# The last stage of a fused decoder kernel: work moved from VectorE to GpSimd and ScalarE, and the next batch's rows prepared between tiles

## The reference, cut to what matters

```python
def _L1_ffn_ref(x, weight, weight_scale, bias):      # x is layernorm(x) here
    amax = jnp.max(jnp.abs(x), axis=-1, keepdims=True)
    x_scale = jnp.maximum(amax, 1e-12) / FP8_MAX     # 448
    qinput = (x / x_scale).astype(FP8)               # float8_e4m3fn
    A = qinput.astype(x.dtype) * x_scale
    Bm = weight.astype(x.dtype) * weight_scale
    return jnp.einsum('bsk,nk->bsn', A, Bm) + bias
```

## Time and profile before

| | us |
|---|---|
| three runs | 3648.0, 3655.38, 3653.69 |
| their median | 3653.69 |
| span of the profiled execution | 3648.2 |
| the last stage in it, from the last residual tile of the fifth (3463.2) to the end | 185.0 |

### The profile page before, as it was taken

One profiled execution on the slowest core, in us unless ns is written; L12 is line 12 of the kernel. 1 busy time (PEld: TensorE's weight loads), 2 busy tenths in 40 slices (PEclk: granted clock), 3 DMA queues, 4 the chain that ended last, 5 costly groups with the idle time before them and its releaser, 6 DMA issues. The chain is left out here.

```text
span 3648.2 us, 78625 instructions
## 1 busy us (share of the span) xinstructions
PE 3088.9 (85%) x31124; PEld 1836.6 (50%) x31124; DVE 2698.1 (74%) x4017; ACT 2360.0 (65%) x4397; POOL 1058.4 (29%) x1854
## 2 busy tenths in 40 slices
PE   6999999978999755899778888998899879998824
PEld 3747474645665543444345554555455545555411
DVE  4748483867897765444469988889888988889688
ACT  3838373766786534333368887778777887788534
POOL 2232323156446234233212222222222222222122
PEclk9999999989999977999999999999999999999956
DMA  4050505175365376344399999999999999999843
GB/s 151 28 146 29 172 5 146 37 249 149 122 201 165 94 251 208 81 119 127 92 220 190 190 199 199 199 202 186 214 196 200 189 214 194 199 201 184 158 158 124
DMA packets 1309823, 582.40 MB, mean 160 GB/s; under 512 B 1144338, under 2 KB 1230994, under 8 KB 1306900
## 3 DMA queue, kind: packets, MB, share of 16 engines
q1 hardware_dynamic: 1305428, 560.60, 69.3%
q0 software_dynamic: 4032, 16.78, 1.2%
HBM read 183.63 MB, written 109.45 MB: 80 GB/s over the span
## 5 line engine op out<-in xcount | busy, mean ns | idle before, releaser
L2296 DVE SCALAR_TENSOR_TENSOR ca_halves<-ca_probs,ca_inv,ca_halves 128x1024 f16<-128x1024 f32 x512 | 655.5, 1280 | 109.9 <-ACT ca_halves L2222 102.4
L2288 DVE TENSOR_REDUCE ca_neg_max<-banks 128x1 f32<-128x1024 f32 x512 | 623.8, 1219 | 64.1 <-PE banks L2066 62.6
L2222 ACT ACTIVATE ca_halves<-ca_probs,ca_inv 128x1024 f16<-128x1024 f32 x512 | 586.6, 1146 | 102.9 <-DMA ca_pt<-ca_halves 99.1
L2214 ACT ACTIVATE ca_probs<-banks,ca_neg_max 128x1024 f32<-128x1024 f32 x512 | 568.7, 1111 | 72.6 <-DVE ca_neg_max L2288 70.7
L2032 POOL TENSOR_SCALAR ca_inv<-ca_total 128x1 f32<-128x1 f32 x512 | 97.5, 190 | 1197.1 <-ACT ca_probs L2214 1197.1
L2066 PE MATMUL banks<-ca_kt,ca_qt 64*128 64x512 f16 x3072 | 381.3, 382 | 48.8 <-ACT ca_probs L2214 47.1
L2088 PE MATMUL banks<-ca_pt,ca_v 128*64 128x256 f16 x6144 | 388.6, 277 | 0.9 <-DMA ca_pt<-ca_halves 0.8
L2088 PEld LDWEIGHTS banks<-ca_pt,ca_v 128*64 128x64 f16 x6144 | 318.6, 111 | 94.2 <-issue 78.4
L2035 POOL TENSOR_TENSOR ca_inv<-ca_inv,ca_minus_one 128x1 f32<-128x1 f32 x512 | 280.3, 548 | 42.6
L2066 PEld LDWEIGHTS banks<-ca_kt,ca_qt 64*128 64x128 f16 x3072 | 132.6, 95 | 238.8 <-issue 95.0
L2047 PE MATMUL banks<-ca_ct,ca_w 128*128 128x512 f16 x768 | 180.5, 386 | 48.1 <-DMA ca_ct<-ctx_part 23.8
(11 more groups left out here) (306 smaller groups left out, 5738.7 us busy)
## 6 DMA issues: line engine op xcount, KB each, us to landing
ca_w<-ca_w_parts SPq DMA_DIRECT2D x32, 768.0 KB, 5.4
wa_v<-v_rows SPq DMA_DIRECT2D x44, 264.0 KB, 4.5
v_rows<-wa_v_stage SPq DMA_DIRECT2D x32, 264.0 KB, 2.2
wa_x<-in_x SPq DMA_DIRECT2D x32, 256.0 KB, 5.3
wa_ring<-in_x SPq DMA_DIRECT2D x32, 256.0 KB, 3.9
x_after_window_attention<-wa_ring SPq DMA_DIRECT2D x32, 256.0 KB, 3.1
ba_tokens<-wa_tok_turned SPq DMA_DIRECT2D x32, 256.0 KB, 3.6
ba_xt<-ba_tokens SPq DMA_DIRECT2D x32, 256.0 KB, 7.2
```

What stands on the lines that cost most here:

```text
L2214: act.activation(probs[:, slot, :], scores(i), ACT.Exp, bias=neg_max[:, slot:slot + 1], accum_out=total[:, slot:slot + 1]).then_inc(exped, 1)
L2222: act.activation(halves[:, slot, 0, :], probs[:, slot, :], ACT.Copy, scale=inv[:, slot:slot + 1]).then_inc(split_hi, 1)
L2288: dve.tensor_reduce(out=neg_max[:, slot:slot + 1], in_=scores(i), axis=X_AXIS, op=ALU.max, negate=True).then_inc(maxed, 1)
L2296: dve.scalar_tensor_tensor(out=halves[:, slot, 1, :], in0=probs[:, slot, :], scalar=inv[:, slot:slot + 1], in1=halves[:, slot, 0, :], op0= ...
```

## The change

All of it lies in `fp8_ffn`. One block takes the place of two. Slots become `FF_SLOTS` = 4, `xn` and the scales hold two batches, and four PSUM banks take the transposes instead of two.

- GpSimd writes the normalised rows, with add and mult of two pointer scalars (a negated mean, made in one more small instruction, and the inverse deviation), widens the 8-bit rounding to bfloat16 (a `tensor_copy`), and adds the bias in the turn to which it belongs.
- ACT makes the shifted row and takes the constant off again, the latter one turn later and straight into `q`. The square is gone.
- DVE marks by the exponent bits of the 8-bit value (one bitwise AND on bytes), and COPY_PREDICATED puts the widened value over `q` where they aren't zero.
- The next batch's work lies between the turns: DVE takes `norm_stats` of two tiles in each of turns 0 to 3, and the maxima of two in each of turns 4 to 7; GpSimd makes two tiles of rows in each of turns 4 to 7.
- SyncE loads a tile of the batch after the next behind each store, where it loaded the next batch's eight in one run.
- The weights are decoded in the same block, behind the statistics of batch 0.

```diff
 @block.sync
+    for t in range(NT):
+        sp.dma_start(n.x[:, t, :], tokens_in(x_in, 0, t)).then_inc(n.x_loaded[t], 16)
+    sp.dma_start(bits8 ...); sp.dma_start(w_scale ...); sp.dma_start(bias ...)
...
+    for t in range(NT):
+        sp.wait_ge(n.xn_ready, t + 1)
+        sp.dma_start(n.x[:, t, :], tokens_in(x_in, 1, t)).then_inc(n.x_loaded[t], 16)
     for b in range(B):
-        if b + 1 < B:
-            sp.wait_ge(n.xn_ready, NT * (b + 1))
-            for t in range(NT):
-                sp.dma_start(n.x[:, t, :], tokens_in(x_in, b + 1, t)).then_inc(n.x_loaded[t], 16)
         for t in range(NT + 1):
             if t < NT:
                 sp.wait_ge(n.res_ready, NT * b + t + 1)
                 sp.dma_start(tokens_in(x_out, b, t), n.ring[:, t, :]).then_inc(n.stored[t], 16)
+            if b + 2 < B and t >= 1:
+                sp.wait_ge(n.xn_ready, NT * (b + 1) + t)
+                sp.dma_start(n.x[:, t - 1, :], tokens_in(x_in, b + 2, t - 1)).then_inc(n.x_loaded[t - 1], 16)
             if t >= 1 and b + 1 < B:
                 sp.wait_ge(n.stored[t - 1], 16 * b + 16 * (n.turn + 1))
                 sp.dma_start(n.ring[:, t - 1, :], tokens_in(x_in, b + 1, t - 1)).then_inc(n.ring_loaded[t - 1], 16)
 @block.gpsimd
+    def moments(b):
+        pool.wait_ge(n.moments, 2 * NT * (b + 1))
+        pool.tensor_scalar(neg_mean[:, :], n.mv[:, :, 0], -1.0, 1.0, ALU.mult, ALU.mult).then_inc(centred, 1)
+        norm_gpsimd(pool, n, b)
...
+    def rows(b, t):
+        pool.tensor_scalar(xn[:, b % 2, t, :], n.x[:, t, :], neg_mean[:, t:t + 1], n.rstd[:, t:t + 1],
+                           ALU.add, ALU.mult).then_inc(n.xn_ready, 1)
+    def widen(b, t):
+        turn = NT * b + t
+        pool.wait_ge(coarsened, turn + 1)
+        if turn >= FF_SLOTS:
+            pool.wait_ge(merged, turn - FF_SLOTS + 1)
+        pool.tensor_copy(wide[:, turn % FF_SLOTS, :], coarse[:, turn % FF_SLOTS, :]).then_inc(widened, 1)
...
+    for b in range(B):
+        for t in range(NT):
+            widen(b, t)
+            if b + 1 < B and t == NT // 2:
+                if b >= 1:
+                    pool.wait_ge(merged, NT * b)
+                moments(b + 1)
+            if b + 1 < B and t >= NT // 2:
+                rows(b + 1, 2 * t - NT)
+                rows(b + 1, 2 * t - NT + 1)
+            add_bias(b, t)
 @block.scalar
+    def grids(b, t):
...
+        act.wait_ge(scaled, b + 1)
+        act.activation(coarse[:, s, :], xn[:, b % 2, t, :], ACT.Copy, scale=half_inv[:, b % 2, t:t + 1], saturate=False)
...
+        act.activation(rounded[:, s, :], xn[:, b % 2, t, :], ACT.Identity, bias=rounder[:, :],
+                       scale=half_inv[:, b % 2, t:t + 1]).then_inc(added, 1)
+    def finer(turn):
...
+        act.activation(q[:, s, :], rounded[:, s, :], ACT.Identity, bias=unround[:, :]).then_inc(fined, 1)
+    for turn in range(NT * B):
+        grids(*divmod(turn, NT))
+        if turn >= 1:
+            finer(turn - 1)
+        if turn >= 2:
+            evacuate(turn - 2)
 @block.vector
+    def mark(b, t):
+        dve.wait_ge(coarsened, NT * b + t + 1)
+        dve.tensor_scalar(is_normal[:, s, :], coarse[:, s, :].bitcast(U8), EXPONENT, None, ALU.bitwise_and).then_inc(marked, 1)
+    def merge(b, t):
+        dve.wait_ge(fined, turn + 1)
+        dve.wait_ge(widened, turn + 1)
+        dve.wait_ge(marked, turn + 1)
+        dve.memset(fences[:, 1:2], 0.0)
+        dve.copy_predicated(q[:, s, :], is_normal[:, s, :], wide[:, s, :]).then_inc(merged, 1)
...
+    for b in range(B):
+        for t in range(NT):
+            turn = NT * b + t
+            mark(b, t)
+            if b + 1 < B:
+                if t < NT // 2:
+                    norm_stats(dve, n, b + 1, 2 * t)
+                    norm_stats(dve, n, b + 1, 2 * t + 1)
+                else:
+                    largest_of(b + 1, 2 * t - NT)
+                    largest_of(b + 1, 2 * t - NT + 1)
+                if t == NT // 2 - 1:
+                    norm_aggregate(dve, n, b + 1)
+                if t == NT - 1:
+                    scales(b + 1)
+            merge(b, t)
+            if turn >= 3:
+                residual(turn - 3)
```

More of the change, by code:

```diff
@@ L2339 @@
 ROUNDER = 1.5 * 2.0 ** 13
-FINE_BELOW = 2.0 ** -6
+EXPONENT = 0x78
+FF_SLOTS = 4
 def fp8_ffn(nc, consts, psum, x_in, x_out, dram):
@@ L2352, in fp8_ffn @@
+        neg_mean, amax = sb("ff_neg_mean", [P, NT], F32), sb("ff_amax", [P, NT], F32)
+        x_scale, grid_scale = sb("ff_x_scale", [P, 2, NT], F32), sb("ff_grid_scale", [P, 2, NT], F32)
+        half_inv, out_scale = sb("ff_half_inv", [P, 2, NT], F32), sb("ff_out_scale", [P, 2, NT], F32)
         fences = sb("ff_fences", [P, 4], F32)
[L2353 to L2356, removed]
@@ L2365, in fp8_ffn @@
-        flipped, flip_out, projected = sem("ff_flipped"), sem("ff_flip_out"), sem("ff_projected")
[L2366 to L2376, removed]
-                    for t in range(NT):
[L2378 to L2386, removed]
@@ L2519, in _, with project @@
                 norm_aggregate(dve, n, 0)
+                dve.wait_ge(constant, 2)
+                decode()
+                dve.wait_ge(scale_loaded, 16)
+                for t in range(NT):
+                    largest_of(0, t)
+                scales(0)
                 for b in range(B):
-                    rows(b)
-                    shift(b, 0)
                     for t in range(NT):
-                        if t + 1 < NT:
-                            shift(b, t + 1)
+                        turn = NT * b + t
+                        mark(b, t)
                         if b + 1 < B:
-                            norm_stats(dve, n, b + 1, t)
-                        merge(b, t)
-                        if t >= 2:
-                            residual(b, t - 2)
-                        if b + 1 < B and t == NT - 1:
-                            norm_aggregate(dve, n, b + 1)
-                    for t in range(NT - 2, NT):
-                        residual(b, t)
+                            if t < NT // 2:
[8 more added lines that the diff above has]
+                                scales(b + 1)
+                        merge(b, t)
+                        if turn >= 3:
+                            residual(turn - 3)
+                for turn in range(NT * B - 3, NT * B):
+                    residual(turn)
             @block.tensor
             def _(pe):
-                def project(b, t):
-                    if NT * b + t >= 4:
-                        pe.wait_ge(n.res_ready, NT * b + t - 3)
-                    pe.wait_ge(flip_out, NT * b + t + 1)
+                def project(turn):
+                    t = turn % NT
+                    if turn == 0:
+                        pe.wait_ge(decoded, 5)
+                    if turn >= 4:
+                        pe.wait_ge(n.res_ready, turn - 3)
+                    pe.wait_ge(flip_out, turn + 1)
                     for k in range(KC):
```

223 lines of the change are left out of this document (110 added, 113 removed).

## The result

| us | before | after |
|---|---|---|
| median of the runs | 3655.38 (5 runs, 3648.0 to 3660.06) | 3636.41 (5 runs, 3631.28 to 3647.25) |
| ratio of after to before, 95% interval | | 0.9956 (0.9940 to 0.9972) |
| profiled execution: own time, span | span 3648.2 | 3635.97, 3634.2 |
| last residual tile of the fifth stage | 3463.2 | 3464.7 |
| last stage, from there to the end (difference of the unrounded times) | 184.9 | 169.5 |

The interval is 10 to 22 us faster. The profiled executions differ by 14.0 us in span: the last stage is 15.4 us shorter, and the five stages that nobody touched came out 1.5 us longer.

A forecast was written before the change was run, and what follows sets the result against it. DVE was taken to bound the last stage. Periods saving 12.1 us and the head 9.1, less 1.2 lost in the last batch, gave 20.0 us off the median: 3634 us, range 3608 to 3672.

The forecast's parts named there:

- POOL's rows: Normalised rows on GpSimd, turns 4 to 7 and head: 0.62 us each with add and mult, not 2.07 as with subtract.
- The slower rival: GpSimd's rows cost 2.07 us in turns 4 to 7 and the head; time 3680 us; chance 0.20.
- The first half of a period: From half_inv through turns 0 to 3 to the statistics' aggregate, set by DVE: 16.4 us.
- the seam: Between two batches: three ACT instructions after half_inv, before DVE's merge of the last turn can start, 2.0 us.
- The second half: Turns 4 to 7, aggregate to half_inv: set by GpSimd's chain with DVE hidden, 17.0 us.
- The port: DVE's mark and predicated copy wait for GpSimd's running instruction: 0.39 us each, 0.8 us a turn.
- The moved loads: Loads of x behind stores make DVE's statistics in turns 2 and 3 wait: 4.0 us in batches 1 and 2.
- Batch 0: First of three periods, half_inv to half_inv, without waits for moved loads: 33.4 us against 40.1.
- The head: Start of the last stage up to the first half_inv, with no block end behind the loads: saves 9.1 us.
- The last batch: From the last half_inv to the end, no next batch: 33.0 us against 31.8, loses 1.2.
- small interference: Rival: port and loads hardly bite, turns of 2.8 us, periods of 28.3; time 3608 us; chance 0.10.
- a restarting seam: Rival: each period's seam restarts all engines, some 6 us more each; time 3652 us, no change; chance 0.08.

The follow-up runs named there:

- e2: Changed kernel with GpSimd's rows made by subtract of the mean and mult instead of add of the negated mean and mult; median 3680.91 us, ratio to before 1.0067.
- e1: Changed kernel with the loads of x for tiles 3 to 7 issued together behind tile 4's store; last stage 157.2 us, ratio to before 0.9907.
- e3: Changed kernel with GpSimd's bias added to only the first of 512 features, the rest left out; last stage 150.8 us, ratio to before 0.9899.
- e6: Changed kernel with the 8-bit weights loaded and decoded ahead of batch 0's statistics, still in one block; last stage 172.4 us, ratio to before 0.9965.

## Why the prediction was right, and where its sizes were off

The forecast was 3634, the median 3636.41. The steps did less well than the sum: 20.0 us were forecast for the stage, and 15.4 came in the profiled executions. The medians lie 19.0 apart, 3.6 more than the stage saved; that is within the 7 us by which whole times vary, so that the total came this near is in part luck.

**POOL's rows: right, and on the right ground.** The argument was that a pointer is the same for a whole row, so that the excess of 1.45 us had to be the subtraction's. e2 bears it out: with subtract a row costs 2.07 again (the tile of the scalar, which changed with it, apart). The price of add and mult is 0.76, not 0.62, which makes 8 x 0.14 = 1.1 us a period. The Trainium skill, GPSIMD Engine Reference, section 4.1, has one-input elementwise work here at roughly line-rate. The trace comes near that for add and mult (0.77 us a row of 512 elements, where DVE had taken 0.54 before the change) and contradicts it for subtract and mult (2.07), so the rule could not have decided the case. The slower rival, with its place and its 3680, was priced well: e2 gave 3680.91.

**The first half of a period: right without the loads.** Forecast 16.4 us, 16.5 in e1. Its inner terms moved against each other: the seam took 2.3, not 2.0, ACT's shifted row being 0.80 us where I had at most 0.71 from the earlier trace rows; merge and residual behind it took 1.6, not 1.3, that copy being held (1.01); the three turns took 10.4 in e1 (distances of the copies 3.13, 4.06, 3.18), forecast 10.8; the rest took the 2.3 of the forecast.

**The second half: 1 us low.** Forecast 17.0, measured 17.9. Several sizes were off and partly cancelled: the rows 1.1 more; the negated mean 0.50 us instead of 0.2, which with the waits makes 0.4 more; behind the last row 0.3 more, the first short scale instruction being held (0.50 us, 0.17 in e3); against that POOL lost some 2.1 us at the port, not 2.8, and a bias costs 1.20 from start to start, not 1.26. That POOL would set it and DVE be hidden was right (the 3.99 us turns without a gap on POOL).

**The port: right in kind, smaller in the mean.** I took 0.39 us for each of mark and copy. Their means are 0.26 and 0.24 over the clean price, and most of it is POOL's bias, as e3 shows (0.08 and nothing are left without it). The Trainium skill, SBUF — State Buffer, "SBUF: two separate sides", says that of a DVE instruction in a 2-port mode, or with two SBUF inputs (then only against a GpSimd one that reads SBUF), and a GpSimd one, the first to start has the shared ports for its whole length and the other blocks. The trace agrees, in both directions: the copy at 3548.59 ended 0.55 us after the bias did, and the widening at 3549.11 took 1.07 us. The two prices of L1795 in the earlier trace rows fit as well: POOL worked beside both, but in the one of 2.29 us it started 1.0 us after DVE (1450.35 and 1451.36). The mark, with one input, is held as well, up to 1.50 us, which fits the first kind; no run shows in which mode it ran.

**The moved loads: the step that failed, by its size.** Forecast 4.0 us a period, measured 6.6 in waits and 6.3 by e1. The chain was as put, and from the residual to the landing it took 3.2 and 3.3 us for tiles 5 and 6, forecast 3.4. The error was in what DVE does meanwhile: I had let the mark wait 0.8 us at the port there, and it did not (0.41 and 0.42), so tile 5's statistic stood 2.2 instead of 1.6 and tile 6's 3.0 instead of 2.2. Tile 7's load, issued behind a store and two other loads, took 4.0 us from issue to landing, and 1.4 stood in place of 0.3. I had used the same port wait as a cost in one step and as cover in the next, though it need not fall in the turn where cover is wanted.

**Batch 0: not seen.** 31.0 us against 33.4. In its first three turns there is no residual yet (3 x 0.66 = 2.0) and no merge of a turn before at its seam; from half_inv to the next aggregate it took 13.0 us, where e1's other periods took 16.5. I had counted all periods alike.

**The head: 1.2 us short of its gain.** 25.0 us where 23.8 was forecast. The last aggregate was on time; from there to half_inv it took 11.4, forecast 9.8; 1.1 of the difference is the price of a row. The timeline of the changed kernel:

```profile
3477.75 0.54 DVE L325 BATCH_NORM_AGGREGATE ff_mv<-ff_stats 128x2 f32<-128x6 f32 x7
3478.21 1.19 DVE L2494 CAST ff_bits<-ff_bits 128x2048 uint16<-128x2048 uint8 x1
3478.38 1.08 POOL L2410 TENSOR_SCALAR ff_neg_mean<-ff_mv 128x8 f32<-128x8 f32 x1 [10.31 <-DVE ff_mv L325]
...
3479.71 2.00 POOL L311 TENSOR_TENSOR ff_rstd<-ff_rstd,minus_half 128x8 f32<-128x8 f32 x1
...
3481.89 6.46 POOL L2417 TENSOR_SCALAR ff_xn_all<-ff_x,ff_neg_mean,ff_rstd 128x512 f32<-128x512 f32 x8 [0.19 <-POOL ff_rstd L311]
...
3489.52 0.20 DVE L2520 RECIPROCAL ff_half_inv<-ff_grid_scale 128x8 f32<-128x8 f32 x1
```

The negated mean, a 128x8 instruction, took 1.08 us beside the decode's first instruction of 1.19, the power 2.00 instead of 1.65, and the rows 6.46 instead of 5.0.

**The last batch: 31.9, not 33.0.** Its first merge ended 0.9 us later than forecast (in part the seam again), its seven turns took the 18.2 of the forecast, and the end was cheaper: 7.8 us from the last merge, where I kept the 9.7 of before. TensorE now has four banks for the transposes instead of two, which I take for the reason; no run tested it.

**In sum**, forecast against measured savings: periods 12.1 and 7.7 (batches 1 and 2 each 3.4 longer than forecast, 2.4 of it by the loads and 1.0 by the second half, and batch 0 2.4 shorter), head 9.1 and 7.9, last batch a loss of 1.2 and of 0.1. The rivals of small interference and of a restarting seam did not come; but the seam was real money, 2.8 us a period, and one exchanged pair of calls on ACT takes it out.

## What to carry to other kernels

When a load is tied to a store, count from the work that releases the store to the tile's use, and let only work that surely falls there be cover; a wait that costs in the sum is no cover in the schedule. Before work goes to GpSimd, find the price of that very operation with its kinds of scalars: here one sign, moved into a small instruction, decided between 0.4% faster and 0.7% slower. When a batch boundary makes an engine wait, look at the order of calls on it: what belongs to the old batch should stand ahead of what waits for the new one.

## What the runs showed of the hardware that was not expected

- On GpSimd, a 128x512 float32 TENSOR_SCALAR with two pointer scalars takes 0.77 us for add and mult, and 2.07 for subtract and mult (the first scalar then read from another tile).
- On ScalarE, a 128x512 activation with a pointer for the bias and one for the scale took 0.80 us; those with one of the two took 0.71 (means of 32: 802, 713 and 710 ns).

```profile
L2469 ACT ACTIVATE ff_rounded<-ff_xn_all,ff_rounder,ff_half_inv 128x512 f32<-128x512 f32 x32 | 25.7, 802 | 0.0
L2465 ACT ACTIVATE ff_coarse<-ff_xn_all,ff_half_inv 128x512 fp8e4<-128x512 f32 x32 | 22.8, 713 | 54.4 <-DVE ff_half_inv L2520 54.4
L2477 ACT ACTIVATE ff_q<-ff_rounded,ff_unround 128x512 bf16<-128x512 f32 x32 | 22.7, 710 | 0.0
```

- Small GpSimd instructions are held too: the negated mean (128x8) took 1.08 us beside the decode, 0.50 to 0.58 in the other three instances, and 0.21 in e6, where the decode had gone before it.
- Stages that no edit touched ended up to 14 us apart between executions (3458.7 to 3472.7), as much as the change brought.
